# Grouped attentions of a four-layer network: the steps of the main loop issued in twos

## The chip, the core and the metric

The kernel runs on one core of a Trainium2 chip. The metric is the device time of one execution in microseconds. Five engines work from queues of their own and meet through semaphores: TensorE (PE in the profile; its weight loads are PEld), VectorE (DVE), ScalarE (ACT), GpSimd (POOL), and SyncE (SP), which issues DMAs. The time before the change is the median of three runs.

## The reference, cut to what matters

Four layers, each an attention and a feed-forward part, on x of 4 x 512 x 256. The changed function serves the attentions of layers 1, 2 and 3. Layers 1 and 2 are causal, layer 2 with rotary embedding; the third has no mask and a scrambled assignment of heads to rows.

```python
x = x + attn(layernorm(x))          # layers 1, 2: causal; layer 3: no mask
# in attn, per batch of 512 positions, 16 heads of 16 dimensions:
q, k, v = split(x @ Wqkv)
s = einsum('gqd,gkd->gqk', q, k) * norm
p = softmax(s, axis=-1)
ctx = einsum('gqk,gkd->gqd', p, v)
out = ctx @ Wproj + bias
```

## The kernel before

`attention_quads` computes an attention in a loop of FULL = 4 x 32 = 128 steps, 32 per batch. A batch has four groups of four heads; a group takes 8 steps, namely four tiles of 128 keys, each for two pairs of heads.

Each head pair lies in the 128 partitions as two halves of 64 rows. Per step TensorE does:

- `scores_T(N)` (L1212, matmul L1223, causal masks L1228 and L1232): the transposed scores, keys by queries, of two heads, one per half of the array, 64 rows by 128 columns. Even steps write banks 0 and 1 of PSUM, odd steps banks 2 and 3. ScalarE turns them into exponentials (L1150) in `pT`.
- `scores(t)` for two tiles t = 2N + 24 and 2N + 25 (L1193, matmul L1203, masks L1206 and L1208), also 64 by 128: queries by keys, only for the row maxima, which VectorE takes (L979, `maxima`). They are needed as extra rows of q some steps later. Tile `a` = 0 or 1 writes bank 4 + a, so tile t may start only when the maximum of tile t - 2 is taken: `pe.wait_ge(max_done, t - 1)`.
- at odd steps `values(J)` (L1236, matmul L1246): the products with the values for two steps back, on the array cut into four parts of 32 columns (128 by 32), into bank 6. ScalarE copies bank 6 out after four of them (`leave`, L1106).
- one `piece`, by a table `plan` over the 32 steps, on the full array (128 by 128), always through bank 7: "turn" (L1166, input transposed), "project" (L1178 to L1180), "values" (L1188 to L1190), "maxima" (L1254, the maxima transposed, then stored into q by ScalarE L1084 and VectorE L984), "group" (L1260, the finished group transposed back, then L992 and L994), "heads" (L1267) and "outputs" (L1278 or L1281, then added by VectorE L1012). A piece first waits until the piece before it has left bank 7 (`freed`).

Per step the order on TensorE before is: transposed scores, scores, values (odd steps), piece. In the table, the even steps with a piece are for attention 1: 2, 6, 8, 10, 12, 14, 16, 18, 22, 24, 30; for attention 2 also 4; for attention 3: 0, 2, 6, 8, 10, 12, 14, 16, 18, 20, 22, 24, 30. Pieces for the next batch are missing in the last batch and pieces of the batch before in the first.

In the causal attentions only the needed part is computed. Scores tiles are 256 keys wide at steps n with n mod 8 = 0 and 1, then 128, 512 and 384 for the next twos; the transposed scores at the same steps have 512, 384, 256 and 128 queries. A "pair" below is an even step and the odd step behind it.

GpSimd splits projected inputs into a high and a low part (`split_kept`, L923 and L925, 2.5 us together) and splits the maxima (`split_maxima`, L931 to L941) at the steps with N % 8 == 4. The order of the work on each engine is just the order of its loop in the code; nothing schedules it.

Of the kernel before, what the change touches and what calls it, by code (L numbers as in the profile page):

```python
# [16 lines left out]
KC = D // P  # L17
# [676 lines left out]
def attention_quads(nc, tag, X, Y, cst, PS, scr, filled, weights, masks=None, rope=None, bias=None, scrambled=False):  # L694
# [15 lines left out]
    with ExitStack() as ctx:  # L710
# [66 lines left out]
        def piece_at(N):  # L777

            kind, ahead, i = plan.get(N % STEPS, ("none", 0, 0))
            b = N // STEPS + ahead  # L780
            return (kind, b, i) if 0 <= b < NB else ("none", 0, 0)

        def previous_piece(N):
            return next((p for p in (piece_at(n) for n in range(N - 1, -1, -1)) if p[0] != "none"), ("maxima", 0, 0))

# [5 lines left out]
        def queries_from(kt):  # L791
            return kt * P if causal else 0
# [27 lines left out]
        def kept_index(b, i):  # L820
            return KEPT * (b - 1) + i
# [6 lines left out]
        with nc.Block() as block:  # L828
# [56 lines left out]
            def _(pool):  # L885
# [11 lines left out]
                def rotated(b, u):  # L897

                    pool.wait_ge(sin_done, NU * b + u + 1)
                    pool.tensor_tensor(comp[:, u % 2, 0, :], comp[:, u % 2, 0, :], comp[:, u % 2, 1, :], ALU.add).then_inc(comp_done, 1)  # L900

                def lower(b, u):

                    pool.wait_ge(unit_high[u], b + 1)
                    if b:
                        pool.wait_ge(wrote[u], 48 * b)
                    pool.tensor_tensor(low[:, u, :], comp[:, u % 2, 0, :], high[:, u, :].bitcast(F32),
                                       ALU.subtract).then_inc(unit_low[u], 1)

                def split_kept(b, i):  # L910

                    c = kept_index(b, i)
                    src = full[:, c % 2, :]
                    pool.wait_ge(kept, c + 1)
                    if i < KC:
                        hi, lo, hi_sem, lo_sem, value = xnT[:, i, :], x_low[:, i, :], split_x, x_done, KC * b + i + 1
                        pool.wait_ge(proj_done, NU * rot * b)
                        pool.wait_ge(v_done, TB // 2 * b)
                    else:
                        u = i - KC  # L920
                        hi, lo, hi_sem, lo_sem, value = high[:, u, :], low[:, u, :], unit_high[u], unit_low[u], b + 1
                        pool.wait_ge(wrote[u], 48 * b)
                    pool.tensor_tensor(hi, src, zeros[:, :], ALU.add).then_inc(hi_sem, 1)  # L923
                    pool.wait_ge(hi_sem, value)
                    pool.tensor_tensor(lo, src, hi.bitcast(F32), ALU.subtract).then_inc(lo_sem, 1)  # L925
# [25 lines left out]
                    for t in range(NT):  # L951
                        pool.tensor_tensor(Y[:, t, :], X[:, t, :], bb[:, :], ALU.add).then_inc(y_started, 1)
                for N in range(FULL):
                    kind, b, i = piece_at(N)
                    if kind == "turn":
                        split_kept(b, i)
                    elif kind == "project" and rope is None:
                        split_kept(b, KC + i)
                    elif kind == "project" and i % 2:
                        rotated(b, i // 2)  # L960
                        lower(b, i // 2)
                    if N % STEPS == 25 and N // STEPS + 2 < NB:
                        layer_norm_pool(pool, ln, N // STEPS + 2, neg_half)
                    if N % 8 == 4 and N // 8 + 1 < NB * NG:
                        split_maxima(N // 8 + 1)

            @block.vector
            def _(dve):
                def source(c):
                    return lambda t: X[:, TB * c + t, :]  # L970
# [44 lines left out]
                def piece(kind, b, i):  # L1015
                    if kind == "maxima":
                        keep_maxima(b, i)
                    elif kind == "group":
                        finish_group(b, i)
                    elif kind == "project" and rope is not None:  # L1020
                        rotate(b, i, 7)
                    elif kind == "outputs":
                        add_outputs(b, i)
# [28 lines left out]
                for N in range(FULL):  # L1052
                    for t in (2 * N + LEAD, 2 * N + LEAD + 1):
                        if t < NB * TILES_:
                            maxima(t)
                    piece(*piece_at(N))
                    if N % STEPS == 24 and N // STEPS + 2 < NB:
                        layer_norm_stats(dve, ln, N // STEPS + 2, source(N // STEPS + 2))
                    if N % STEPS == 26 and N // STEPS + 2 < NB:
                        dve.wait_ge(transposed, KC * (N // STEPS + 2))  # L1060
                        layer_norm_apply(dve, ln, N // STEPS + 2, source(N // STEPS + 2))
# [4 lines left out]
            def _(act):  # L1066
# [41 lines left out]
                def piece(kind, b, i):  # L1108
                    if kind == "maxima":
                        keep_maxima(b, i)  # L1110
                    elif kind == "turn":
                        keep(b, i, (transposed, KC * b + i + 1))
                    elif kind == "project" and rope is None:
                        keep(b, KC + i, (proj_done, NU * b + i + 1))
                    elif kind == "project" and i % 2:
                        upper(b, i // 2)
                    elif kind == "values":
                        keep_values(b, i, 7)
                    elif kind == "heads":
                        keep_heads(b, i)  # L1120
# [23 lines left out]
                for N in range(FULL):  # L1144
                    b, n = N // STEPS, N % STEPS
                    q0 = queries_from(n % 8 // 2)
                    act.wait_ge(st_done, N + 1)
                    if N >= 4:
                        act.wait_ge(pv_done, N // 2 - 1)
                    act.activation(pT[:, N // 2 % 2, N % 2, :, q0:S], PS[:, 2 * (N % 2):2 * (N % 2) + 2, q0:S], ACT.Exp,  # L1150
                                   scale=SCALE).then_inc(exp_done, 1)
                    if N % 8 == 2 and N >= 10:
                        leave((N - 10) // 8)
                    piece(*piece_at(N))
                leave(NB * NG - 1)
                for p in LAST:
                    piece(*p)
# [2 lines left out]
            def _(pe):  # L1160
# [163 lines left out]
                for u in range(NU):  # L1324
                    pe.wait_ge(unit_low[u], 1)
                for N in range(FULL):
                    scores_T(N)
                    for t in (2 * N + LEAD, 2 * N + LEAD + 1):
                        if t < NB * TILES_:
                            scores(t)  # L1330
                    if N % 2 and N >= 3:
                        values((N - 3) // 2)
                    piece(*piece_at(N), previous_piece(N))
                values(FULL // 2 - 1)
# [1397 lines left out]
```

## Time and profile before

| | us |
|---|---|
| median of 3 runs (2102.32 to 2106.85) | 2105.98 |
| the profiled execution | 2110.35 |
| its span in the trace | 2108.6 |
| TensorE busy, matmuls | 1676.1 (79%) |
| VectorE busy | 1247.2 (59%) |
| ScalarE busy | 976.2 (46%) |
| GpSimd busy | 517.3 (25%) |
| DVE L979, maxima, 768 instructions | 395.8 |
| ACT L1150, exponentials | 308.5 |

The three loops lie at about 621 to 876, 1071 to 1337 and 1646 to 1932 us. A matmul's start is measured, but its end is modelled, so neighbouring matmuls overlap in the rows; what one costs is read from start to start. A row of the timeline merges equal instructions (x2, x4). In the profile the granted clock of TensorE is 1.00 (2.4 GHz) or 0.50 (1.2 GHz).

### The profile page before, as it was taken

To read this page: it belongs to the slowest core of one execution; us is meant where nothing else is said; L and a number is where in the kernel's file an instruction comes from. 1 tells how busy PE (TensorE), PEld (TensorE's weight loads), DVE (VectorE), ACT (ScalarE), POOL (GpSimd) and SP (SyncE) were. 2 spreads that over 40 slices of the span, in tenths; PEclk is the share of its full clock that TensorE was granted. 3 is DMA by queue.
4 is the path that set the end of the run, shared out by engine and by line. 5 is a ranking of instruction groups with operands and counts; after the bars stand their busy time and mean duration, and the time that the engine had idled before them with its cause. 6 is when DMAs were issued, how large, how long until landed. Compare 5 with 4: busy or idle time off the path is not lost. (4 is left out here: it accounts for less than half of the span.)

```text
span 2108.6 us, 30346 instructions
## 1 busy us (share of the span) xinstructions
PE 1676.1 (79%) x10966; PEld 1042.3 (49%) x10966; DVE 1247.2 (59%) x2607; ACT 976.2 (46%) x1533; POOL 517.3 (25%) x567
## 2 busy tenths in 40 slices
PE   3899999689879999701499999668986899996776
PEld 2455555378755555401355555446764344442543
DVE  2566667333245566399556656247774777783555
ACT  1677879533124444300124445337661455664422
POOL 4121100023222330020322230037892422300000
PEclk8799999899969999855679999769997799998688
DMA  6242140100055423000433531111114425310101
GB/s 206 59 91 69 38 91 1 60 1 0 18 150 141 127 68 88 25 22 0 124 111 94 141 109 33 68 45 46 46 46 130 102 77 140 106 35 24 45 0 40
DMA packets 62242, 148.48 MB, mean 70 GB/s; under 512 B 9317, under 2 KB 14830, under 8 KB 61210
## 3 DMA queue, kind: packets, MB, share of 16 engines
q1 hardware_dynamic: 62106, 146.69, 25.0%
q8 instruction: 83, 1.36, 0.3%
q14 instruction: 53, 0.43, 0.1%
HBM read 97.29 MB, written 51.45 MB: 71 GB/s over the span
## 5 line engine op out<-in xcount | busy, mean ns | idle before, releaser
L979 DVE TENSOR_REDUCE a_mx<-PS 128x1 f32<-128x512 f32 (+3 forms) x768 | 395.8, 554 | 202.3 <-PE PS L1208 126.4
L1150 ACT ACTIVATE a_pT<-PS 128x1024 f32<-128x1024 f32 (+3 forms) x384 | 308.5, 811 | 222.1 <-PE PS L1232 155.8
L1203 PE MATMUL PS<-a_k,a_q 64*128 64x512 f32 (+3 forms) x768 | 236.6, 445 | 50.1 <-DVE a_mx L979 27.7
L361 DVE CUSTOM_DVE_ANT_0 PS<-PS,a_dist 128x448 f32<-128x448 f32 x256 | 155.2, 649 | 74.1 <-PE PS L592 72.9
L1223 PE MATMUL PS<-a_q,a_k 64*128 64x512 f32 (+3 forms) x768 | 179.3, 451 | 14.8 <-DVE a_q L984 6.1
L1246 PE MATMUL PS<-a_pT,a_va 128*32 128x512 f32 (+3 forms) x1536 | 170.5, 517 | 5.4 <-ACT a_raw L1106 5.4
L1203 PEld LDWEIGHTS PS<-a_k,a_q 64*128 64x128 f32 x768 | 113.2, 204 | 95.8 <-DVE a_mx L979 66.2
L492 ACT ACTIVATE a_p<-PS,a_negm 128x448 f32<-128x448 f32 (+1 forms) x256 | 149.2, 639 | 3.4 <-DVE a_negm L361 1.9
L602 PE MATMUL PS<-cst,a_p 128*128 128x128 f32 x1024 | 144.3, 284 | 4.6 <-DVE a_pT L370 2.0
L2016 DVE TENSOR_TENSOR f_work<-f_work,f_gb 128x512 f32<-128x512 f32 x84 | 109.8, 1334 | 53.0 <-ACT f_work L2104 40.9
L1897 POOL TENSOR_TENSOR f_h_low<-f_work,f_h_high 128x512 fp32r<-128x512 f32 x84 | 130.0, 1572 | 43.9 <-ACT f_h_high L2076 43.2
L1223 PEld LDWEIGHTS PS<-a_q,a_k 64*128 64x128 f32 x768 | 79.2, 193 | 111.9 <-issue 83.6
L602 PEld LDWEIGHTS PS<-cst,a_p 128*128 128x128 f32 x1024 | 111.7, 143 | 38.6 <-issue 33.1
L500 ACT ACTIVATE a_pT<-PS 128x512 f32<-128x512 f32 x205 | 115.2, 604 | 29.8 <-PE PS L602 28.1
L1206 PE MATMUL PS<-a_half_masks 64*128 64x128 bf16 x512 | 90.8, 245 | 0.0
L1084 ACT ACTIVATE a_q<-PS 16x1024 fp32r<-16x1024 f32 x48 | 48.8, 1016 | 87.3 <-PE PS L1254 86.8
L931 POOL TENSOR_TENSOR a_mxh<-a_mx,a_m 128x16 fp32r<-128x16 f32 x48 | 10.9, 228 | 305.8 <-DVE a_mx L979 305.8
L592 PE MATMUL PS<-a_k,a_q 48*128 48x448 f32 x256 | 63.4, 491 | 26.4 <-ACT a_p L492 16.8
L592 PEld LDWEIGHTS PS<-a_k,a_q 48*128 48x128 f32 x256 | 25.2, 192 | 101.0 <-issue 54.8
L1208 PE MATMUL PS<-a_half_masks 64*128 64x64 bf16 x512 | 74.9, 202 | 0.0
L2104 ACT ACTIVATE f_work<-PS,f_b 128x512 f32<-128x512 f32 x84 | 57.4, 683 | 34.6 <-PE PS L2179 34.2
L1178 PE MATMUL PS<-a_xnT,a_w_highqk 128*128 128x512 f32 x128 | 58.8, 459 | 17.4 <-DVE a_x_low L1033 9.7
(348 smaller groups left out, 3602.0 us busy)
## 6 DMA issues: line engine op xcount, KB each, us to landing
spread_scratch<-a_high SPq DMA_DIRECT2D x96, 256.0 KB, 2.3
a_q<-spread_scratch SPq DMA_DIRECT2D x96, 256.0 KB, 5.5
a_k<-spread_scratch SPq DMA_DIRECT2D x96, 256.0 KB, 6.6
spread_scratch<-a_low SPq DMA_DIRECT2D x48, 256.0 KB, 2.6
f_gb<-gate_rows SPq DMA_DIRECT2D x36, 256.0 KB, 5.5
window_scratch<-a_high SPq DMA_DIRECT2D x24, 256.0 KB, 2.2
a_q<-window_scratch SPq DMA_DIRECT2D x32, 192.0 KB, 4.7
a_k<-window_scratch SPq DMA_DIRECT2D x32, 192.0 KB, 5.2
```

Of the source, the lines that this page charges most:

```text
L361: dve.tensor_tensor_reduce(PS[:, bank, 0:KW], PS[:, bank, 0:KW], dt_[:, off:off + KW], float(slopes[2 * pair + a]), 3e38, ALU.add, ALU.min ...
L492: act.activation(p[p0:P, GH * (gg % 2) + i, qt, 0:KW], PS[p0:P, bank, 0:KW], ACT.Exp, bias=negm[p0:P, bank:bank + 1], scale=-1.0).then_inc ...
L500: act.activation(pT[:, J % 2, i, :], PS[:, 4 + e % 2, :], ACT.Copy).then_inc(turned_act, 1)
L602: mm = pe.transpose(PS[:, 4 + e % 2, qt * P:(qt + 1) * P], p[:, GH * (gg % 2) + i, qt, kt * P:(kt + 1) * P], ident)
L979: dve.tensor_reduce(mx[:, gg % 2, qt, 2 * half + a:2 * half + a + 1], PS[:, 4 + a, 0:kw], AX.X, ALU.max).then_inc(max_done, 1)
L1150: act.activation(pT[:, N // 2 % 2, N % 2, :, q0:S], PS[:, 2 * (N % 2):2 * (N % 2) + 2, q0:S], ACT.Exp, scale=SCALE).then_inc(exp_done, 1)
L1203: mm = pe.matmul(ps[:, 0:kw], q[rows, b % 2, pair, qt * P:(qt + 1) * P], k[rows, b % 2, pair, 0:kw], start=True, stop=not causal)
L1206: pe.matmul(ps[:, kw - P:kw], half_masks[rows, 0, 0, :], half_masks[rows, 1, 0, :], start=False, stop=False)
L1223: mm = pe.matmul(PS[:, 2 * half + a, q0:S], k[rows, b % 2, pair, kt * P:(kt + 1) * P], q[rows, b % 2, pair, q0:S], start=True, stop=not ca ...
L1246: mm = pe.matmul(PS[BLK * i:BLK * i + BLK, 6, q0:S], va[:, b % 2, kt, GH * g + i, :], pT[:, J % 2, i // 2, i % 2, q0:S], start=(kt == 0), ...
L1897: pool.tensor_tensor(h_low[:, G % 6, :], prod[:, G % 3, :], h_high[:, G % 6, :].bitcast(F32), ALU.subtract).then_inc(h_low_done, 1)
L2016: dve.tensor_tensor(prod[:, G % 3, :], act_[:, G % 3, :], gb[:, b % 2, e, :], ALU.mult).then_inc(prod_done, 1)
```

## The change

The pieces are no longer issued one per step. At even steps no engine does a piece; at odd steps each does both, first the even step's and then the odd one's. TensorE's order within a pair becomes: the two scores of the even step, the transposed scores of both steps, the two scores of the odd step, the even piece, the values, the odd piece. The same instructions are issued in all; no size, buffer or semaphore changes.

```diff
+        def pieces_at(N):
+
+            return [(n, piece_at(n)) for n in (N - 1, N)] if N % 2 else []
+
...
                 for N in range(FULL):
-                    kind, b, i = piece_at(N)
-                    if kind == "turn":
-                        split_kept(b, i)
...
+                    for n, (kind, b, i) in pieces_at(N):
+                        if kind == "turn":
+                            split_kept(b, i)
...
-                    piece(*piece_at(N))
+                    for n, x in pieces_at(N):
+                        piece(*x)
...
                 for N in range(FULL):
-                    scores_T(N)
+                    if N % 2:
+                        scores_T(N)
                     for t in (2 * N + LEAD, 2 * N + LEAD + 1):
                         if t < NB * TILES_:
                             scores(t)
-                    if N % 2 and N >= 3:
+                    if N % 2 == 0:
+                        scores_T(N)
+                        continue
+                    piece(*piece_at(N - 1), previous_piece(N - 1))
+                    if N >= 3:
                         values((N - 3) // 2)
                     piece(*piece_at(N), previous_piece(N))
```

The middle part (`for n, x in pieces_at(N)`) stands in VectorE's and in ScalarE's loop alike. Eleven lines are added to the file, so L979 of before is L983, L1203 is L1209, L1223 is L1229, L1246 is L1252 and L1278 is L1284.

TensorE's order in the third attention before, steps 2 and 3 of a middle batch (`a_q,a_k` are the transposed scores, `a_k,a_q` the scores, `a_pT,a_va` the value products, the others pieces):

```order
L1223 MATMUL PS<-a_q,a_k 128x512 x2
L1203 MATMUL PS<-a_k,a_q 128x512 x2
L1166 MATMUL PS<-cst,a_ln_xn 128x128 x4
L1223 MATMUL PS<-a_q,a_k 128x512 x2
L1203 MATMUL PS<-a_k,a_q 128x512 x2
L1246 MATMUL PS<-a_pT,a_va 32x512 x4
L1260 MATMUL PS<-cst,a_raw 128x128 x4
```

The same steps in the changed kernel:

```order
L1209 MATMUL PS<-a_k,a_q 128x512 x2
L1229 MATMUL PS<-a_q,a_k 128x512 x4
L1209 MATMUL PS<-a_k,a_q 128x512 x2
L1172 MATMUL PS<-cst,a_ln_xn 128x128 x4
L1252 MATMUL PS<-a_pT,a_va 32x512 x4
L1266 MATMUL PS<-cst,a_raw 128x128 x4
```

The piece that stood between the two parts of scores now stands behind both, and the value products lie between the two pieces.

GpSimd's order in the first attention before, steps 8 to 12 of a batch (`a_high` and `a_low` are one projection's split, `a_mxh` and `a_m` the split of the maxima):

```order
L923 TENSOR_TENSOR a_high<-a_full,a_zeros 128x512
L925 TENSOR_TENSOR a_low<-a_full,a_high 128x512
L923 TENSOR_TENSOR a_high<-a_full,a_zeros 128x512
L925 TENSOR_TENSOR a_low<-a_full,a_high 128x512
L931 TENSOR_TENSOR a_mxh<-a_mx,a_m 128x16
```

And in the changed kernel:

```order
L927 TENSOR_TENSOR a_high<-a_full,a_zeros 128x512
L929 TENSOR_TENSOR a_low<-a_full,a_high 128x512
L935 TENSOR_TENSOR a_mxh<-a_mx,a_m 128x16
L944 TENSOR_TENSOR a_m<-a_mxh,a_m 128x4x2x2
L945 TENSOR_TENSOR a_m<-a_mx,a_mxh 128x4x2x2
L927 TENSOR_TENSOR a_high<-a_full,a_zeros 128x512
L929 TENSOR_TENSOR a_low<-a_full,a_high 128x512
```

The split of the maxima of step 12 now stands ahead of the last projection's split instead of behind it.

## Rows read from the trace of the kernel before

**Rows 1.** Windows, third loop: length, busy PE, PEld, DVE, ACT, POOL, clock, DMA
```profile
1646.00:1932.00 286.00, 263.68 (x1476) 122.53 (x1476) 204.05 (x336) 173.29 (x200) 60.81 (x90) 0.98 0.29 78
```
**Rows 2.** Timeline, PE, third attention, pair with outputs piece: start, us, instruction
```profile
1721.18 0.50 PE L1223 MATMUL PS<-a_q,a_k 64*128 64x512 f32 x2
...
1722.03 1.13 PE L1278 MATMUL PS<-a_wo,a_aT 128*128 128x256 f32 x4
1723.09 0.50 PE L1223 MATMUL PS<-a_q,a_k 64*128 64x512 f32 x2
...
1723.74 1.06 PE L1246 MATMUL PS<-a_pT,a_va 128*32 128x512 f32 x8
1724.74 0.66 PE L1166 MATMUL PS<-cst,a_ln_xn 128*128 128x128 f32 x4
```
**Rows 3.** Timeline, PE, third attention, pair without even piece
```profile
1903.86 0.50 PE L1223 MATMUL PS<-a_q,a_k 64*128 64x512 f32 x2
1904.19 0.62 PE L1203 MATMUL PS<-a_k,a_q 64*128 64x512 f32 x2
1904.43 0.62 PE L1223 MATMUL PS<-a_q,a_k 64*128 64x512 f32 x2
1905.37 1.09 PE L1203 MATMUL PS<-a_k,a_q 64*128 64x512 f32 x2 [0.32 <-DVE a_mx L979]
1906.39 1.06 PE L1246 MATMUL PS<-a_pT,a_va 128*32 128x512 f32 x8
```
**Rows 4.** Timeline, DVE, the same stretch
```profile
1904.62 2.56 DVE L979 TENSOR_REDUCE a_mx<-PS 128x1 f32<-128x512 f32 x4 [0.36 <-PE PS L1203]
```
**Rows 5.** Timeline, PE, third attention, scores behind a short even piece
```profile
1718.27 0.92 PE L1203 MATMUL PS<-a_k,a_q 64*128 64x512 f32 x2
1719.12 1.06 PE L1246 MATMUL PS<-a_pT,a_va 128*32 128x512 f32 x8
```
**Rows 6.** Timeline, PE, from a projection to the transposed scores
```profile
1745.19 0.39 PE L1179 MATMUL PS<-a_x_low,a_w_highqk 128*128 128x512 f32 x1
1745.42 0.40 PE L1180 MATMUL PS<-a_xnT,a_w_lowqk 128*128 128x512 f32 x1
1745.75 0.50 PE L1223 MATMUL PS<-a_q,a_k 64*128 64x512 f32 x2
```
**Rows 7.** Timeline, PE, first attention, scores 512 wide, no even piece
```profile
834.10 0.38 PE L1223 MATMUL PS<-a_q,a_k 64*128 64x256 f32 x2
...
834.40 0.48 PE L1203 MATMUL PS<-a_k,a_q 64*128 64x512 f32 x2
...
834.81 0.37 PE L1223 MATMUL PS<-a_q,a_k 64*128 64x256 f32 x2
...
836.95 0.85 PE L1246 MATMUL PS<-a_pT,a_va 128*32 128x384 f32 x8
```
**Rows 8.** Timeline, PE, first attention, scores 384 wide, maxima piece
```profile
837.73 0.33 PE L1223 MATMUL PS<-a_q,a_k 64*128 64x128 f32 x2
...
838.42 0.66 PE L1254 MATMUL PS<-cst,a_m 128*128 128x128 f32 x4
839.00 0.33 PE L1223 MATMUL PS<-a_q,a_k 64*128 64x128 f32 x2
...
840.07 0.64 PE L1246 MATMUL PS<-a_pT,a_va 128*32 128x256 f32 x8
```
**Rows 9.** Groups by shape, DVE, 600 to 1940: busy, mean ns, idle before
```profile
L984 DVE TENSOR_SCALAR a_q<-PS 16x1024 fp32r<-16x1024 f32 x48 | 59.0, 1229 | 16.0 <-PE PS L1254 14.8
...
L1012 DVE TENSOR_TENSOR Y<-Y,PS 128x512 f32<-128x512 f32 x32 | 22.0, 688 | 15.1 <-PE PS L1278 14.5
```
**Rows 10.** Timeline, first attention, step 14 of a batch: POOL and PE
```profile
718.07 1.27 POOL L925 TENSOR_TENSOR a_low<-a_full,a_high 128x512 fp32r<-128x512 f32 x1
...
720.14 0.93 PE L1254 MATMUL PS<-cst,a_m 128*128 128x128 f32 x4 [1.42 <-POOL a_m L941]
```
**Rows 11.** Windows, behind that wait: the columns of rows 1
```profile
720.40:730.50 10.10, 10.10 (x67) 6.26 (x66) 3.76 (x7) 4.05 (x5) 0.00 (x0) 0.50 0.91 259
```

More of the change, by code:

```diff
@@ L953, in _ @@
                 for N in range(FULL):
-                    kind, b, i = piece_at(N)
-                    if kind == "turn":
-                        split_kept(b, i)
[L957 to L961, printed above, removed]
+                    for n, (kind, b, i) in pieces_at(N):
+                        if kind == "turn":
+                            split_kept(b, i)
+                        elif kind == "project" and rope is None:
+                            split_kept(b, KC + i)
+                        elif kind == "project" and i % 2:
+                            rotated(b, i // 2)
+                            lower(b, i // 2)
                     if N % STEPS == 25 and N // STEPS + 2 < NB:
@@ L1153, in _ @@
                         leave((N - 10) // 8)
-                    piece(*piece_at(N))
+                    for n, x in pieces_at(N):
+                        piece(*x)
                 leave(NB * NG - 1)
```

## The prediction

> **What bounds the kernel now.** I read the busy times by window first. In the loops of the three grouped attentions (807 us of the 2108.6) TensorE is busy over nine tenths of the time; the third loop shows it [rows 1]: TensorE 263.68 of 286 us, VectorE 204.05. So TensorE's own sequence sets the pace and every gap between its starts counts; I went on in its timeline, start to start, at granted clock 1.00.
>
> One pair of steps of the third attention [rows 2]: transposed scores, scores (0.85 us from 1721.18 until the piece starts), the even step's piece, transposed scores, scores (0.65 us, 1723.09 to 1723.74), value products (1.00 us), the odd step's piece. I call the time spent in the two 64-row parts H: here 1.50 us.
>
> Where a pair has no even piece, both score parts already follow each other [rows 3]. There two scores start at 1904.19, the transposed ones follow after 0.24, and then TensorE stands until 1905.37, and the value products start at 1906.39. H is 2.53, though the same matmuls need 0.33 + 0.24 + 0.23 + 0.32, some 1.1 (estimate from the starts of unhindered neighbours). VectorE meanwhile reduces four tiles without a pause, 2.56 us from 1904.62 [rows 4]. The reason is in the code: `scores(t)` waits until the maximum of tile t-2 is taken, since two tiles share banks 4 and 5. This is the row on which my forecast rests. A short even piece covers only part of that [rows 5]: scores from 1718.27 until 1719.12, 0.85 where an unhindered part takes 0.33; H is 1.95.
>
> **What the change removes.** Per pair with an even piece the sequence half, full, half, column, full becomes half, full, column, full: one change of array shape less. Its price: full-array matmuls of 512 columns start 0.23 apart, the first half-array one after them 0.33 later [rows 6], and its follower again 0.33 later (the first two starts of [rows 3]) instead of 0.23. Together 0.20. The trace holds no change from full to 32 columns in these rows; I take the same 0.09 on leaving (between nothing and 0.20). From the plan: 36, 39 and 44 such pairs, 119 in all, so 24 us gross.
>
> The Trainium skill, page "TensorEngine Tiling (Array Packing)", section "Key Properties", says that changing the tiling mode drains TensorE; the 0.10 before the shape changes agrees. The section "PSUM Bottleneck" of the same page warns that a faster TensorE leaves the emptying of PSUM as the bound, and that speaks against this change; by the first rule alone the time would fall by 24 us, by the second it rises.
>
> **What it adds: the maxima have no cover.** Every pair now runs scores, transposed x2, scores. The first two scores free their banks only after 1.29 us of VectorE (half of the four tiles in [rows 4]), and only the two transposed products (0.46) lie between. From the first score to the value products [rows 3] is 1906.39 - 1904.19 = 2.20; as the first of its shape it pays 0.10 more: H = 2.30 in every pair.
> - Third attention, long even piece (outputs, project, values), 25 pairs: 2.30 - 1.50 = +0.80, 20 us.
> - Short even piece (four transposes), 17 pairs: 2.30 - 1.95, 6 us.
> - No even piece, 16 pairs: 2.30 - 2.53, -4 us.
> In the two causal attentions the tile width depends on the phase:
> - Width 512: chained, 834.40 to 836.95 is 2.55 [rows 7], plus 0.10 is 2.65. With an even piece it is now 2 x (0.30 + 0.41 + 0.09 for leaving) and a little waiting, 1.67. 9 pairs, +0.98, 9 us.
> - Width 384, always with the short piece of the maxima: now 0.69 + 1.07 = 1.76 [rows 8]. Then: entry 0.10; first reduction 0.55 after the start (0.43 in [rows 3, 4] and the mask products); two reductions of 0.5, three quarters of the 0.64 of [rows 4] and a little; restart 0.06; last score 0.45 (0.69 less 0.24 for the transposed products [rows 8]); about 2.2, an estimate. 28 pairs, 13 us.
> - Widths 256 and 128: the reductions are shorter (half and a quarter of the elements) and the transposed products longer, so they are almost covered; 45 pairs, +2 us.
> - Pairs without an even piece: -4 us.
> Sum of the H parts: +42 us, net of the saved switches.
>
> **What the moved pieces add.** Pieces of both steps share bank 7 and now have only the value products between them.
> - The odd piece waits for the emptying of the even one: 0.11 until it starts, 0.69 on VectorE (L1012) or 0.60 on ScalarE, 0.07 until TensorE goes, 0.87 or 0.78 against value products of 0.36 to 1.00. After the maxima piece it is 0.11 + 1.23 + 0.07 = 1.41 (L984) [rows 9]. Third attention: 13 output pieces wait 0.4 to 0.5, 6.5 us. Causal: 12 projections and outputs x 0.45, the values piece of step 23 six times 0.55, and the turned group at step 3, behind two exponentials, the raw copy and the copy of the even piece on ScalarE, four times 0.5: with the smaller ones 10 us.
> - On VectorE the odd piece's work stands just ahead of the next pair's maxima and ends 0.80 after the piece, while the first maximum could start 0.53 after it: 0.27 late, 26 pairs in the third (7 us), in the causal ones 4 us. Layer norm statistics at step 24 of two batches: 2 us.
> These sum to +29.5 us.
>
> **What goes away.** GpSimd now handles pieces at odd steps only, so the split of the maxima at step 12 stands ahead of the split of projection 12. Before, that split ended at 719.34 and the maxima's transposes came with 1.42 us idle [rows 10]. Six places (step 14, first and third attention): 3 x 1.9 + 3 x 1.3, start to start, since the idle time of a row begins only at a modelled end. At step 4 of the second, twice, a projection waits 1.8 for the lower half of x; the longer H covers it. 13 us. Where no odd piece follows, value products no longer carry the wait for the stored maxima: -6 us. Right behind the stall of rows 10 the granted clock is 0.50 from 720.4 to 730.5 [rows 11], the 1.2 GHz level; three such stretches in the first attention cost about 9 us against the same steps at 2.4 GHz, two in the second 2. With their stalls gone they may stay warm, but the new gaps could bring others: between -11 and +36 (a fall in each batch of each attention, 12 x 3 us), I take -7.
>
> **The sum.** 42 + 29.5 - 13 - 6 - 7 = +45.5 us. The profiled execution took 2110.35 and would become 2156; the median of the runs is 2105.98, so I forecast 2151. No DMA is on this path: stores and fetches of the next batch hang on the projections, which move later by about 1.4 us, and the transfers have the same number of steps, each now longer, to land. If that cover were gone, step 20 would wait there.
>
> **Rivals.**
> 1. Only the switch counts (faster). If the bank release were early enough for the second pair of scores, -24 from the switches, -13 from GpSimd, -7 of clock: 2062. For it: TensorE is the bound [rows 1] and the switches are real [rows 6]. Against it: rows 3 show this very sequence stalling. It decides if the reduction of one tile were below 0.25 us. 6 in 100.
> 2. The causal stages break even, the third pays. Their estimates for 384 columns and for ScalarE's queue are the least direct. Dropping the 13 and two thirds of the 16 us of moved pieces gives +22: 2128. 20 in 100.
> 3. The clock falls often. Each pair of the third now idles about 1.1 us in 5.5; if the granted clock drops as at 720.4 once per batch, up to +36 instead of -7: 2185. For: [rows 11]. Against: chained pairs follow each other in the last batch at 1.00, with 1.1 idle in 4.1. 15 in 100.
> 4. The gains and waits cancel by chance (2095 to 2112): 4 in 100.
> My own case has 55 in 100, with its own range of 2135 to 2172.
>
> **Numbers.** 2115 to 2183 holds my case, most of rival 2 and part of rival 3. Within 0.2% (4 us, about what a measurement of this kernel can tell from no change): 0.03. Faster: 0.07, rival 1 with a bit of rival 4. Slower: 0.90.
>
> **What would show it.** In the changed profile: scores, four transposed products, then a score with idle time before it that a maximum (VectorE) ended, in every pair; 2.3 us from the first score of a pair to the piece in the third attention; pairs of the third loop near 5.5 instead of 4.6 us, its loop 30 to 38 us longer; the first attention's loop about level, the second's 10 us longer; no wait of the maxima's transposes for GpSimd. Outside the loops nothing changes. I am wrong if the second scores start together right behind the transposed ones, or if the odd pieces don't wait for bank 7.

## The result, and the profile after

The changed kernel took 2142.11 us (median of 4 runs, 2138.75 to 2146.36), the kernel before in the same comparison 2106.41: 35.7 us slower, ratio 1.017 with an interval of 1.0141 to 1.0198. The forecast was 2151. The profiled execution took 2138.75 us, 28.4 more than that of before; sums over rows are compared with this difference.

The first lines of its page, with the groups that answer to L979 and L1203 of before (busy time, mean ns, idle time ahead and what ended most of it), and behind them the line of L1203 from the page of before:

```profile
span 2136.9 us, 30346 instructions
PE 1673.9 (78%) x10966; PEld 1044.6 (49%) x10966; DVE 1234.0 (58%) x2607; ACT 964.8 (45%) x1533; POOL 515.5 (24%) x567
...
L983 DVE TENSOR_REDUCE a_mx<-PS 128x1 f32<-128x512 f32 (+3 forms) x768 | 393.1, 552 | 185.3 <-PE PS L1214 117.1
...
L1209 PE MATMUL PS<-a_k,a_q 64*128 64x512 f32 (+3 forms) x768 | 264.6, 469 | 71.0 <-DVE a_mx L983 42.5
```

```profile
L1203 PE MATMUL PS<-a_k,a_q 64*128 64x512 f32 (+3 forms) x768 | 236.6, 445 | 50.1 <-DVE a_mx L979 27.7
```

The same instructions are busy for about the same time (TensorE 1673.9 us against 1676.1, the other engines within 1.2%), yet the span is longer: TensorE stands more. The idle time ahead of the scores rises from 50.1 to 71.0 us, and the part of it that a maximum ended from 27.7 to 42.5. Idle time counts only from a modelled end of the matmul ahead, so it is less than what the starts show; for the weight loads of the same scores the part that a maximum ended goes from 66.2 to 130.9.

The windows of the three loops, from the first to the last transposed scores, then the stretch of [rows 11], which ran at the 1.2 GHz level before; columns as in [rows 1]:

```profile
623.60:871.50 247.90, 222.05 (x2312) 137.47 (x2314) 139.19 (x309) 123.38 (x188) 57.33 (x85) 0.99 0.34 90
1063.90:1339.30 275.40, 245.88 (x2382) 151.77 (x2383) 154.73 (x333) 121.70 (x187) 57.35 (x85) 0.98 0.30 81
1646.60:1954.60 308.00, 271.57 (x1442) 126.07 (x1442) 199.55 (x331) 168.29 (x196) 60.09 (x89) 0.98 0.27 72
...
720.40:730.50 10.10, 9.10 (x84) 6.07 (x82) 3.46 (x11) 4.43 (x6) 0.63 (x3) 1.00 0.72 228
```

Measured the same way the loops of before took 255.0, 268.4 and 277.2 us. So the first is 7.1 shorter, the second 7.0 and the third 30.8 longer; outside the loops the profiled executions differ by 2.3, the other way. Added up from start to start over the whole third loop, the 64-row score parts took 121.8 us before and take 145.1, the value products with the waits behind them 62.7 and 72.3, the pieces 89.7 and 88.9. So 23.3 of the 30.8 us lie in the score parts.

TensorE's timeline of a pair of the third attention with the maxima and an output piece, and VectorE's beside it (start, us, instruction, idle time and releaser):

```profile
1763.78 0.51 PE L1209 MATMUL PS<-a_k,a_q 64*128 64x512 f32 x2
1764.11 0.64 PE L1229 MATMUL PS<-a_q,a_k 64*128 64x512 f32 x4
1765.06 1.10 PE L1209 MATMUL PS<-a_k,a_q 64*128 64x512 f32 x2 [0.31 <-DVE a_mx L983]
1766.09 0.66 PE L1260 MATMUL PS<-cst,a_m 128*128 128x128 f32 x4
1766.67 1.06 PE L1252 MATMUL PS<-a_pT,a_va 128*32 128x512 f32 x8
1768.24 1.10 PE L1284 MATMUL PS<-a_wo,a_aT 128*128 128x256 f32 x4 [0.51 <-ACT a_q L1089]
1769.28 0.50 PE L1209 MATMUL PS<-a_k,a_q 64*128 64x512 f32 x2
```

```profile
1764.31 2.57 DVE L983 TENSOR_REDUCE a_mx<-PS 128x1 f32<-128x512 f32 x4 [2.90 <-PE PS L1209]
```

H, from 1763.78 to the piece at 1766.09, is 2.31 (forecast 2.30; before 1.50, [rows 2], or 1.95, [rows 5]). It is 2.30 or 2.31 in 22 of the 58 pairs that have scores, and 2.42 to 2.52 in 30 more, which the next rows explain. The output piece starts 1.57 after the value products, which need 1.00. The pair takes 5.50. VectorE reduces four tiles without a pause just as in [rows 4], now also in pairs with an even piece.

Behind an odd output or transposing piece VectorE is late as well, here behind the transposed group, whose division ends at 1842.3. PE, then DVE:

```profile
1841.79 0.63 PE L1229 MATMUL PS<-a_q,a_k 64*128 64x512 f32 x4
1842.93 1.09 PE L1209 MATMUL PS<-a_k,a_q 64*128 64x512 f32 x2 [0.51 <-DVE a_mx L983]
```

```profile
1842.19 2.56 DVE L983 TENSOR_REDUCE a_mx<-PS 128x1 f32<-128x512 f32 x4
```

The second scores start 1.14 after the transposed ones instead of 0.95, since the piece's work stands ahead of the maxima: 0.20 late where 0.27 was forecast.

The first attention at step 14, where [rows 10] show 1.42 us of idle time. GpSimd, then PE:

```profile
712.88 0.23 POOL L945 TENSOR_TENSOR a_m<-a_mx,a_mxh 128x16 f32<-128x16 f32 x1
```

```profile
717.74 0.66 PE L1260 MATMUL PS<-cst,a_m 128*128 128x128 f32 x4
...
719.77 0.50 PE L1229 MATMUL PS<-a_q,a_k 64*128 64x512 f32 x2 [0.38 <-ACT a_q L1089]
```

The maxima are split at 713.1, long before TensorE transposes them, and the wait is gone. The last row shows a wait that I had not forecast: the next group's transposed scores wait until ScalarE has stored the maxima, because the maxima piece now stands behind the second scores, and only the value products and one part of scores lie between it and them. A second such wait is at the value products: in the first and in the second attention they wait nine times each for ScalarE's copy of bank 6 (L1111), 6.6 us of idle time in each, where it was 2.0 before.

### The profile page after: what moved, and what is told of

It reads as the page before. It is cut to its first block and busy times, and to the rows that moved or that the text cites. A ratio compares the mean times of both kernels' runs of the same rounds, so it can differ in the third digit from the quotient of the medians.

```text
span 2136.9 us, 30346 instructions
## 1 busy us (share of the span) xinstructions
PE 1673.9 (78%) x10966; PEld 1044.6 (49%) x10966; DVE 1234.0 (58%) x2607; ACT 964.8 (45%) x1533; POOL 515.5 (24%) x567
## 5 line engine op out<-in xcount | busy, mean ns | idle before, releaser
L983 DVE TENSOR_REDUCE a_mx<-PS 128x1 f32<-128x512 f32 (+3 forms) x768 | 393.1, 552 | 185.3 <-PE PS L1214 117.1
L1155 ACT ACTIVATE a_pT<-PS 128x1024 f32<-128x1024 f32 (+3 forms) x384 | 295.4, 810 | 232.9 <-PE PS L1238 151.5
L1209 PE MATMUL PS<-a_k,a_q 64*128 64x512 f32 (+3 forms) x768 | 264.6, 469 | 71.0 <-DVE a_mx L983 42.5
L1209 PEld LDWEIGHTS PS<-a_k,a_q 64*128 64x128 f32 x768 | 115.5, 197 | 204.4 <-DVE a_mx L983 130.9
L1252 PE MATMUL PS<-a_pT,a_va 128*32 128x512 f32 (+3 forms) x1536 | 166.2, 505 | 15.1 <-ACT a_raw L1111 14.6
L1229 PE MATMUL PS<-a_q,a_k 64*128 64x512 f32 (+3 forms) x768 | 138.3, 402 | 12.8 <-ACT a_q L1089 9.3
L2027 DVE TENSOR_TENSOR f_work<-f_work,f_gb 128x512 f32<-128x512 f32 x84 | 104.6, 1265 | 59.2 <-ACT f_work L2115 45.9
L1229 PEld LDWEIGHTS PS<-a_q,a_k 64*128 64x128 f32 x768 | 78.9, 190 | 25.5 <-ACT a_q L1089 12.9
```

The source lines that it names most:

```text
L983: dve.tensor_reduce(mx[:, gg % 2, qt, 2 * half + a:2 * half + a + 1], PS[:, 4 + a, 0:kw], AX.X, ALU.max).then_inc(max_done, 1)
L1209: mm = pe.matmul(ps[:, 0:kw], q[rows, b % 2, pair, qt * P:(qt + 1) * P], k[rows, b % 2, pair, 0:kw], start=True, stop=not causal)
L1229: mm = pe.matmul(PS[:, 2 * half + a, q0:S], k[rows, b % 2, pair, kt * P:(kt + 1) * P], q[rows, b % 2, pair, q0:S], start=True, stop=not ca ...
L1252: mm = pe.matmul(PS[BLK * i:BLK * i + BLK, 6, q0:S], va[:, b % 2, kt, GH * g + i, :], pT[:, J % 2, i // 2, i % 2, q0:S], start=(kt == 0), ...
L2027: dve.tensor_tensor(prod[:, G % 3, :], act_[:, G % 3, :], gb[:, b % 2, e, :], ALU.mult).then_inc(prod_done, 1)
```

## The experiments

My theory: TensorE is bound by when banks 4 and 5 are released; grouping two pairs of scores takes the cover away. The rivals: the waits for bank 7 carry the loss, VectorE's or GpSimd's order does, or the clock.

**Short maxima, in both orders.** Line L983 (L979):

```diff
-  dve.tensor_reduce(mx[...], PS[:, 4 + a, 0:kw], AX.X, ...)
+  dve.tensor_reduce(mx[...], PS[:, 4 + a, 0:64], AX.X, ...)
```

> The changed kernel with each row maximum taken over the first 64 columns only (the rest is left out), so that VectorE frees banks 4 and 5 in about 0.2 us instead of up to 0.64. Theory (the maxima have no cover): the second scores of a pair follow the transposed ones at once, H in the third attention falls from 2.30 to about 1.15 us in 58 pairs (-67 us), in the causal ones by 0.6 to 1.4 us in some 75 pairs (-80 us); about 2000 us. Rival (bank 7 or ScalarE's queue behind the adjacent pieces carries the loss): the odd pieces' waits stay and the time stays above 2100.

> The kernel before with the same shortened maxima. Theory: only the pairs without an even piece or with a short one waited for maxima; 17 x 0.5 + 16 x 1.1 us in the third attention and some 38 us in the causal ones go: about 2041. The order of the two kernels turns round: with short maxima the changed one is faster by the switches and the GpSimd order, some 30 to 40 us. Rival: the changed one stays slower than this one by about as much as now.

Measured: 2037.15 us (ratio 0.9695, 0.9674 to 0.9715) in the changed order and 2032.2 (0.9655, 0.9635 to 0.9675) in that of before. The gap shrinks from 36 to 5 us (8 by the ratios), so the length of the maxima carries some 30 of the 36. But the changed order doesn't turn out faster, as I had expected: about 2000 against 2041 was the expectation, and its first half missed by 37 us. PE and DVE of the changed order, and last the second of the two scores that start the first row:

```profile
1735.89 0.62 PE L1209 MATMUL PS<-a_k,a_q 64*128 64x512 f32 x2
1736.44 0.66 PE L1260 MATMUL PS<-cst,a_m 128*128 128x128 f32 x4
```

```profile
1735.61 0.35 DVE L983 TENSOR_REDUCE a_mx<-PS 128x1 f32<-128x64 f32 x2 [1.78 <-PE PS L1209]
```

```profile
1736.02 0.49 PE L1209 MATMUL PS<-a_k,a_q 64*128 64x512 f32 x1
```

The second scores take 0.55 from start to start where an unhindered part takes 0.33. Their first tile starts at 1735.89, the second 0.13 later, when VectorE is through with its bank too (1735.96), and the piece 0.42 behind that one. Why it is 0.42 and not 0.33 isn't shown. It isn't the first tile: in the changed kernel the second tile starts 0.60 after the first, and the piece follows again 0.42 behind it. The wait for the banks was still there; that led to the next pair of runs.

**No score tile read at all, in both orders.** The maxima come from a constant, and the scores' wait goes with them:

```diff
-  dve.tensor_reduce(mx[...], PS[:, 4 + a, 0:kw], AX.X, ...)
+  dve.tensor_reduce(mx[...], cst[:, C_ID:C_ID + 64], AX.X, ...)
...
-  if t >= 2:
-      pe.wait_ge(max_done, t - 1)
```

> The changed kernel with the maxima taken from a constant tile of 64 columns, so that no score tile is read: banks 4 and 5 need not be emptied, and the waits of the scores for the maxima are gone (the row maxima are left out of the result). With the short maxima the second pair of scores still took 0.56 instead of 0.33 in every pair, since the second tile of the two came late and no longer ran beside the first. Theory: now scores 0.34, transposed products 0.48, scores 0.33, H = 1.15, against 1.43 in the order of before; pairs of the third attention with a projection as even piece 4.3 to 4.4 instead of 4.55; 2005 to 2018 us, some 15 less than the other kernel of this job. What is left against it are the waits for bank 7 behind the maxima piece. Rival: the switches of shape cost nothing by themselves, the pairs stay at 4.5 or above, and the two kernels agree within 5 us.

> The kernel before with the same edit (row maxima left out, no tile of scores read, no wait of the scores for them). Theory: only its pairs without an even piece and the scores 512 wide lose a wait, so it gains little on its short maxima (2032): 2022 to 2030 us, pairs of the third attention with a projection as even piece 4.6 as before. Rival: no difference to the changed order.

Measured: 2002.23 us (0.9523, 0.9507 to 0.9539) and 2002.09 (0.9532, 0.9514 to 0.9551). The pairs are as the theory had them, the total is as the rival had it. PE, changed order (two lines fewer, so L1207 are the scores), a pair with a projection, then the maxima and an output piece:

```profile
1718.07 0.50 PE L1207 MATMUL PS<-a_k,a_q 64*128 64x512 f32 x2
...
1718.87 0.40 PE L1207 MATMUL PS<-a_k,a_q 64*128 64x512 f32 x2
1719.20 0.50 PE L1184 MATMUL PS<-a_xnT,a_w_highqk 128*128 128x512 f32 x1
...
1722.40 0.50 PE L1207 MATMUL PS<-a_k,a_q 64*128 64x512 f32 x2
...
1728.43 1.06 PE L1250 MATMUL PS<-a_pT,a_va 128*32 128x512 f32 x8
1730.53 1.13 PE L1282 MATMUL PS<-a_wo,a_aT 128*128 128x256 f32 x4 [1.03 <-ACT a_q L1089]
```

ScalarE beside the last two rows:

```profile
1727.50 1.94 ACT L1155 ACTIVATE a_pT<-PS 128x1024 f32<-128x1024 f32 x2
1729.46 1.01 ACT L1089 ACTIVATE a_q<-PS 16x1024 fp32r<-16x1024 f32 x1
```

PE in the order of before, a pair with a projection, and VectorE, which empties bank 7 of the group's transposes:

```profile
1716.14 0.50 PE L1221 MATMUL PS<-a_q,a_k 64*128 64x512 f32 x2
...
1716.80 1.07 PE L1244 MATMUL PS<-a_pT,a_va 128*32 128x512 f32 x8
...
1718.39 0.50 PE L1221 MATMUL PS<-a_q,a_k 64*128 64x512 f32 x2
...
1719.27 0.50 PE L1178 MATMUL PS<-a_xnT,a_w_highqk 128*128 128x512 f32 x1
...
1720.86 0.50 PE L1221 MATMUL PS<-a_q,a_k 64*128 64x512 f32 x2
```

```profile
1718.79 0.42 DVE L994 TENSOR_TENSOR a_at<-PS,a_rs 128x256 f32<-128x256 f32 x1
```

H is 1.13 in the changed order and 0.66 + 0.88 = 1.54 in the other, the pair 4.33 against 4.72. These 0.4 us are of two kinds. Two unhindered parts of the old order take 2 x 0.66 = 1.32, as ahead of the value products at 1716.80, so the saved change of shape gives 0.19. The rest is a wait for bank 7: the projection at 1719.27 starts once VectorE has left the bank, at 1719.21. In the order of before an even piece starts only 0.76 (ScalarE empties), 0.85 (outputs) or 0.88 (group) after the piece ahead has ended, where the part of scores between them needs 0.66.

The gain is given back behind the maxima piece: two exponentials stand ahead of the storing of the maxima on ScalarE, and the odd piece starts 2.10 after the value products instead of 1.00. The third loop, at a mean clock of 0.99 in both, shows the exchange: from start to start the score parts add up to 82.7 us against 100.1, the value products with the waits behind them to 79.5 against 62.6, and the loops are level (252.9 and 253.0). The first loop is 10.3 us shorter in the changed order (clock 0.98 against 0.91), the second 10.7 longer (0.94 against 0.97).

With the waits for banks 4 and 5 gone the two orders are level; with them they are 36 us apart. So these 36 us hang on the maxima. Two limits stay. The edit also takes VectorE's time for the maxima from 393 to 132 us, so release and load of VectorE aren't told apart. And the changed order carries GpSimd's order too, worth some 10 us by itself (below); in the order of before the maxima piece still waits 12.1 us for GpSimd. Grouping alone would thus still cost some 10 us here, an estimate from these numbers.

**The even piece back between the scores, on TensorE alone** (from the changed kernel):

```diff
                         scores_T(N)
+                        piece(*piece_at(N - 1), previous_piece(N - 1))
...
-                    piece(*piece_at(N - 1), previous_piece(N - 1))
                     if N >= 3:
```

> The changed kernel, but TensorE issues the odd step's two scores behind the even piece: scores, transposed x2, even piece, scores, values, odd piece. The switch comes back, the maxima get their cover back; all other engines keep the changed order. Theory: the long pairs' H is back at 1.5 us, 2080 to 2092 (before, less GpSimd's order and the clock). Rival (the paired pieces on VectorE and ScalarE cost the time): stays above 2125.

Measured: 2169.11 us, 1.0325 (1.0298 to 1.0353), a miss of 80 us. PE, then DVE:

```profile
1888.27 0.59 PE L1209 MATMUL PS<-a_k,a_q 64*128 64x512 f32 x2
1888.79 1.07 PE L1252 MATMUL PS<-a_pT,a_va 128*32 128x512 f32 x8
1890.73 0.50 PE L1184 MATMUL PS<-a_xnT,a_w_highqk 128*128 128x512 f32 x1 [0.88 <-DVE Y L1016]
1892.34 0.50 PE L1209 MATMUL PS<-a_k,a_q 64*128 64x512 f32 x2
```

```profile
1888.80 1.29 DVE L983 TENSOR_REDUCE a_mx<-PS 128x1 f32<-128x512 f32 x2 [0.49 <-PE PS L1209]
1890.00 0.68 DVE L1016 TENSOR_TENSOR Y<-Y,PS 128x512 f32<-128x512 f32 x1
```

The scores at 1888.27 hardly wait any more (0.52 from start to start, 0.33 unhindered), and the pair that begins at 1892.34, with the values as even piece, takes 4.52, where the changed kernel needs 5.50. That part of the theory holds; the time came out on the side of the rival. VectorE's queue still has the even piece's work behind the odd maxima, though the piece is done early: bank 7 is emptied only at 1890.7, and the odd piece starts 0.94 after the value products end. The first attention fell to a mean clock of 0.88 with it. The rival had named VectorE's and ScalarE's paired pieces, and here it is VectorE's queue.

**VectorE in that order too** (even piece, odd maxima, odd piece):

```diff
+                    if N % 2:
+                        piece(*piece_at(N - 1))
                     for t in (2 * N + LEAD, 2 * N + LEAD + 1):
...
-                    for n, x in pieces_at(N):
-                        piece(*x)
+                    if N % 2:
+                        piece(*piece_at(N))
```

> The run with the odd scores behind the even piece (2169 us) once more, but VectorE now follows TensorE: even piece, the odd step's maxima, odd piece. Theory 1 (that run lost its gain because VectorE emptied bank 7 only behind the odd maxima: value products 1.95 and 2.36 instead of 1.00 long where an outputs or maxima piece stood before them): these waits go, the third loop falls from 296 to 255 to 270, and with GpSimd's order the kernel lands at 2060 to 2095. Theory 2 (adjacent transposed scores load ScalarE, whose copies come late whatever VectorE does): above 2125.

Measured: 2115.96 us, 1.0045 (1.0028 to 1.0062), between the two expectations. By the medians 53 us (59 by the ratios) came back from the order of one engine's queue. What is left against before, its PE and ACT show (L1254 are the value products here):

```profile
1868.86 1.06 PE L1254 MATMUL PS<-a_pT,a_va 128*32 128x512 f32 x8 [0.59 <-ACT a_raw L1113]
```

```profile
1868.12 0.59 ACT L1113 ACTIVATE a_raw<-PS 128x512 f32<-128x512 f32 x1
```

In pairs without a piece the value products wait for the copy of bank 6 at 1868.12, which stands behind an exponential. How the remaining 10 us split between this and colder clock (0.95, 0.91 and 0.94 in its loops) stays open.

**The value products ahead of both pieces** (changed kernel, `values` moved above the even piece, two lines swapped):

```diff
-                    piece(*piece_at(N - 1), previous_piece(N - 1))
                     if N >= 3:
                         values((N - 3) // 2)
+                    piece(*piece_at(N - 1), previous_piece(N - 1))
```

> The changed kernel with the value products ahead of both pieces: one more switch is saved (119 x 0.20 = -24 us), but the odd piece now waits for the whole emptying of bank 7, 0.78 to 0.87 us, 1.41 behind a maxima piece. Theory (bank 7 is a term of its own): some +25 us net, 2160 to 2175. Rival (bank 7 costs nothing beside the maxima): 2118.

Measured: 2245.5 us, 1.067 (1.0641 to 1.0699). PE:

```profile
1918.26 1.13 PE L1284 MATMUL PS<-a_wo,a_aT 128*128 128x256 f32 x4
1920.17 0.50 PE L1184 MATMUL PS<-a_xnT,a_w_highqk 128*128 128x512 f32 x1 [0.78 <-DVE Y L1016]
```

The outputs need 1.06 and the next piece starts 1.91 after them. Without the value products in between, the second piece waits 0.75 to 0.85, and 1.4 behind the maxima. The waits have the expected size, but the time is 103 us above the changed kernel's, where some 25 were expected. Added up from start to start, pieces and value products are 67 us longer in the three loops; the score parts of the two causal attentions are 27 longer as well, in the first with the wait for ScalarE's storing of the maxima up from 5.0 to 11.8 us, and that I had not counted at all.

**GpSimd's order alone**, put into the kernel before (`for n, (kind, b, i) in pieces_at(N)` in its loop only), and taken back out of the changed one:

```diff
-                    kind, b, i = piece_at(N)
-                    if kind == "turn":
-                        split_kept(b, i)
+                    for n, (kind, b, i) in pieces_at(N):
+                        if kind == "turn":
+                            split_kept(b, i)
```

> The kernel before with the changed order on GpSimd alone (pieces of both steps at odd steps). Theory: the 1.9 us stall at step 14 of the first attention and the 1.3 us one of the third go, three times each, -9.6 us, and the three stretches at the 1.2 GHz level in the first attention with them, -9 us: 2088 to 2097. Rival (the cold stretches come from elsewhere): 2096, with the granted clock still at 0.50 behind step 14.

> The changed kernel with GpSimd's old order (each step's piece at its own step). Theory: the maxima piece of step 14 waits again for GpSimd, but the longer H covers a part: 3 x 1.1 us in the first attention, 3 x 0.3 in the third, +4 us, and up to 9 more if the clock falls behind the first one: 2146 to 2155. Rival (GpSimd's order is worth nothing): 2142.

Measured: 2092.18 us, 0.9948 (0.9931 to 0.9965), and 2149.69, 1.0216 (1.0192 to 1.024). Both as expected. The first is the fastest of the kernels with whole maxima here, level with the last one below. Windows of its first loop and of the stretch of [rows 11]:

```profile
620.50:863.00 242.50, 229.62 (x2316) 140.16 (x2318) 142.16 (x309) 127.61 (x188) 57.33 (x85) 0.97 0.34 92
720.40:730.50 10.10, 9.46 (x94) 5.62 (x94) 5.71 (x13) 4.09 (x7) 0.63 (x3) 1.00 0.72 219
```

At step 14 the maxima's transposes no longer wait, and no stretch at 1.2 GHz follows: the first attention goes from 255.0 to 242.5. The second goes from 268.4 to 271.0 and the third from 277.2 to 275.9, so the gain is the first attention's.

**Value products at the even step where no even piece stands** (from before), alone and with GpSimd's order:

```diff
-                    if N % 2 and N >= 3:
-                        values((N - 3) // 2)
+                    early = piece_at(N // 2 * 2)[0] == "none"
+                    if N >= 2 and N % 2 == (0 if early else 1):
+                        values(N // 2 - 1)
```

> The kernel before, where in pairs without an even piece the value products stand in its place, between the two scores. Theory: they cover the maxima as a long piece does: ten pairs of the third attention gain up to 1.2 us, 19 pairs with 512 wide scores in the causal ones up to 1.2, eight others 0.5; some is given back where the products wait for the copy of bank 6 or VectorE is short: 2066 to 2086. Rival (the wait only moves): 2106.

> The kernel before with both: GpSimd's order in twos and the value products between the scores of pairs without an even piece. The two act in different pairs, so their gains add: 2052 to 2076 if both do what is expected alone.

Measured: 2112.29 us, 1.0027 (1.0013 to 1.0042), and 2107.14, 1.0004 (0.9985 to 1.0023): two misses. PE and ACT of the first:

```profile
1854.62 1.06 PE L1246 MATMUL PS<-a_pT,a_va 128*32 128x512 f32 x8 [1.25 <-ACT a_raw L1106]
```

```profile
1853.89 0.59 ACT L1106 ACTIVATE a_raw<-PS 128x512 f32<-128x512 f32 x1
```

The maxima are covered (the pair at step 4 of the third attention falls from 4.19 to 3.19), but in the pairs of these rows the value products come too soon after the last ones: bank 6 is still being copied out, behind an exponential, and the pair takes 4.44 instead of 4.12. In the causal attentions the pair at step 6 rises from 3.17 to 4.01. The wait of [rows 3] changed its bank. With both edits GpSimd's order is worth only 5 us, not 11: the gains don't add.

**Scores, transposed x2, scores only where no even piece stands at steps 0 and 4 of a group** (with GpSimd's order):

```diff
-                    scores_T(N)
+                    late = N % 8 in (0, 4) and piece_at(N)[0] == "none"
+                    if not late:
+                        scores_T(N)
...
+                    if late:
+                        scores_T(N)
```

> The kernel before with GpSimd in twos and the changed order of scores (scores, transposed x2, scores) only in pairs without an even piece, at the steps 0 and 4 of each eight. There the maxima had no cover before either. From the pairs of the two traces: step 0 pairs 3.36 -> 2.4 (8 of them, with step 8 of the last batch), step 4 pairs of the causal ones 3.63 -> 3.33 (19), of the third 4.19 -> 4.08 (10); -13 us on the 2092 of GpSimd's order alone: 2075 to 2084. Rival (what such a pair saves, the next one waits for): 2092.

Measured: 2092.72 us, 0.9934 (0.9912 to 0.9955), level with GpSimd's order alone, where the rival had it. The pairs at steps 2 and 4 of the third attention take 8.21 us together against 8.30: grouping costs nothing there, as the scores stood already, and gives next to nothing. In the first attention the pair at step 28 falls from 3.63 to 3.39 and the one at step 30 rises from 3.17 to 3.71, as the rival says. But the clock has a part in it. The profiled execution took 2106.41 us, the longest of eight (2085.19 to 2106.41), and its first attention has a mean clock of 0.91. One of three stretches there:

```profile
689.10:699.20 10.10, 10.10 (x74) 6.10 (x71) 2.32 (x9) 5.24 (x7) 5.48 (x7) 0.50 0.01 2
```

The pair at step 0 begins at 688.20 with a score that waited 0.74 us for a maximum, and the clock is 0.50 right behind it. The pair takes 4.50 instead of 3.36. How much the edit would give without these stretches isn't shown.

## Why the prediction was right, and where its terms were off

**The direction and its cause.** H was forecast as 2.30 from [rows 3], and as 0.27 longer where VectorE is late. In the third attention it is 2.31, and 2.42 to 2.52 in the pairs behind VectorE's late start. The third loop is 30.8 longer (30 to 38 forecast). Of this the score parts make up 23.3; forecast were 22 for H and 7 for VectorE's lateness, less the 3.9 of GpSimd's waits, which lie in the same stretches, so 25. The value products with the waits behind them are 9.6 longer (6.5 forecast for bank 7). The two runs without any read of the score banks show that the maxima are what separates slower from level. The Trainium skill, page "TensorEngine Tiling (Array Packing)", section "PSUM Bottleneck", says that tiling speeds up TensorE but not the emptying of PSUM, which may become the bottleneck. The trace agrees: the idle time ahead of the scores that a maximum ended rose from 27.7 to 42.5 us.

**The price of a switch was right, and too small to matter.** I took 0.20 a pair. Without waits for the score banks it is 2 x 0.66 against 1.13, so 0.19, or some 23 us over 119 pairs, an estimate (24 forecast). What the sum left out is that the even pieces of before waited for bank 7 too, 0.10 to 0.22 a pair, and that the grouped order covers this wait; where H is set by the maxima, as in the third attention, it changed no term, since I took H from measured starts. The Trainium skill, page "TensorEngine Tiling (Array Packing)", section "Key Properties", says that a change of mode drains TensorE; the runs give that a size.

**The moved pieces.** Behind the maxima the wait is 0.57 (forecast 0.4 to 0.5), VectorE is 0.20 late instead of 0.27. These two errors nearly cancel, which is luck: in the third loop 13 x 0.57 + 26 x 0.20 = 12.6 us, against 6.5 + 7.

**The causal attentions were wrong, in their parts and in their sum.** The first should have been about level and the second 10 longer; it was -7.1 and +7.0. Here one step of the prediction failed: "almost covered", +2 us, for scores 256 and 128 wide. In the changed kernel, first attention, PE at step 0 of a batch:

```profile
754.83 0.50 PE L1229 MATMUL PS<-a_q,a_k 64*128 64x512 f32 x2 [0.38 <-ACT a_q L1089]
...
756.02 0.42 PE L1252 MATMUL PS<-a_pT,a_va 128*32 128x128 f32 x8
```

The same step in the kernel before with GpSimd's order:

```profile
748.41 0.51 PE L1227 MATMUL PS<-a_q,a_k 64*128 64x512 f32 x2 [0.20 <-issue]
...
750.83 0.43 PE L1250 MATMUL PS<-a_pT,a_va 128*32 128x128 f32 x8
```

From the transposed scores to the value products it was 2.42 and is 1.19, plus some 0.3 for the scores that now stand ahead. Before, both score parts waited for maxima there; now the first lies behind a piece and the transposed products of two steps, 0.77, cover the rest. About 0.9 us less a pair at step 0 and 0.7 at steps 8 and 16, gains that I had not seen. Against them stands a loss that I had not seen either: the wait for ScalarE's storing of the maxima, of which the row at 754.83 shows 0.38; with it the scores ahead take 0.88 from start to start instead of 0.3. In a whole warm batch of the first attention (687.34 to 754.83, against 683.85 to 748.41 in the kernel before with GpSimd's order) 2.9 us remain as a loss. Scores 512 and 384 wide came out at 2.60 and 2.13 (2.65 and 2.2 forecast). Against the kernel before with GpSimd's order, the score parts of the two attentions add up to 3.3 and 5.6 us more; 20 were forecast for both (9 + 13 + 2 - 4). The waits for the copy of bank 6, 6.6 us in each instead of 2.0, were in no term either.

**GpSimd and the clock.** -13 and -7 were forecast. In the kernel before, GpSimd's order alone gave -11 (ratio 0.9948) with the clock's part in it, and all of it in the first attention (-12.5); in the changed kernel taking it back cost 10 by the ratios, and its first loop went from 247.9 to 258.3. The cold stretches of the first attention are gone, but the second still has two short ones (mean clock 0.75 from 1151 to 1155 and from 1291 to 1295). So both terms together are some 10 us instead of 20.

**The sum.** 45.5 was forecast, 28.4 to 35.7 measured (profile, medians). The forecast's terms give the third attention 22 + 6.5 + 7 - 3.9 = 31.6, and 30.8 came. They leave some 14 for the two causal ones, and -0.1 came: the gain at scores 256 wide outweighed what GpSimd and the clock gave less. With the 2.3 outside the loops this is the 17 us between forecast and profile. Rival 1 (only the switch counts) is refuted for this kernel, and even without any wait for the score banks the changed order is only level: the waits behind the maxima piece take the gain. Rival 3 (the clock falls in each batch) did not happen; the loops have a mean clock of 0.98 and 0.99. Rival 2 comes near in its numbers (causal ones even, +22) for another reason: its terms for 384 columns did come, and a gain stood against them.

## What to carry to other kernels

Before grouping instructions of one array shape, look at what releases their PSUM banks: a piece that costs a switch may be the cover of a reduction. Take the length of the whole chain (matmul, reduction of both tiles, restart) from a place where the profile already shows it without cover, and count every queue in which the releasing instruction stands behind others. A wait taken from banks 4 and 5 came back at bank 7 or at bank 6 in the kernels tried, so look for the next-late bank before expecting the full saving.

## What the runs showed that I had not expected

- Two 64-row matmuls that start together take 0.33 with their change of shape; if the second tile's bank comes free 0.13 later, the two take 0.55. A short lateness of one tile thus costs 0.22, more than itself.
- A queue's order on an engine that is busy for 58% of the span was worth 53 us (2169.11 to 2115.96; 59 by the ratios), more than the change itself.
- The granted clock can fall behind a short stall: with the wait for GpSimd gone (1.9 us start to start, three times in the first attention), the window from 720.4 to 730.5 shows 1.00 where it was 0.50, and the loop is 12.5 us shorter, more than twice the waits themselves. It isn't tied to that wait: with it gone, the clock fell behind a wait of 0.74 us in the last of the experiments. And pairs of the third attention that idle some 1.1 us in 5.5 stayed at 1.00 for the most part (mean 0.98).
